# Moving the input layer norm's last step and the query and key evictions from ScalarE to VectorE in an eight-core transformer layer

## The reference, cut to what matters

```
x = x + layernorm(attn(layernorm(x)))          # x: 8 x 2048 x 1024
x = x + layernorm(ffn(layernorm(x)))

attn(x): q, k, v = x @ Wq, x @ Wk, x @ Wv      # 16 heads of 64, causal, ALiBi bias
         softmax(q k^T / 8 + bias) v @ Wo
ffn(x):  z = layernorm(x) * g + b
         top 2 of 8 experts by softmax(z @ rW), weights w
         x + sum_e w_e * (gelu(z @ W1_e + b1_e) @ W2_e + b2_e)
layernorm(x) = (x - mean) / sqrt(var + 1e-5)
```

## Time and profile before

| what | us |
|---|---|
| median of 3 runs | 3216.63 |
| lowest and highest of them | 3211.04, 3339.13 |
| profiled execution, its own time | 3214.51 |
| span of the profiled execution, slowest core (core 6) | 3213.0 |
| spans of the 8 cores | 3193.7 to 3213.0 |
| TensorE busy in the span | 2759.6 (86%) |
| VectorE busy | 907.9 (28%) |
| ScalarE busy | 1045.9 (33%) |

### The profile page before, as it was taken

The page is one execution under the profiler, slowest core; times in us unless marked ns, Lnnn a source line. Parts: engine busy times, 40 slices in busy tenths (PEclk is TensorE's granted clock), DMA queues, the critical chain, the costliest instruction groups (busy, mean ns, idle before and its releaser), DMA issues.

```text
span 3213.0 us, 40015 instructions; the slowest of 8 cores (3193.7 to 3213.0 us)
## 1 busy us (share of the span) xinstructions
PE 2759.6 (86%) x11328; PEld 1411.6 (44%) x18304; DVE 907.9 (28%) x1765; ACT 1045.9 (33%) x2101; POOL 64.7 (2%) x78
## 2 busy tenths in 40 slices
PE   1988888888988643699999999998599999999996
PEld 1555543222222222345555555554255555555553
DVE  4325244545556456310110011004120011011004
ACT  3313656656655466412112211221202211211221
POOL 0000000000000000000000000000000000000000
PEclk9996555555555676799999999999799999999998
DMA  5111000000000532436335543644726534634542
GB/s 145 27 27 27 1 1 1 1 1 1 1 1 1 111 132 105 107 58 105 66 58 88 85 73 53 105 79 108 148 34 105 79 58 75 105 62 62 87 79 92
DMA packets 92893, 205.06 MB, mean 64 GB/s; under 512 B 4248, under 2 KB 12568, under 8 KB 92704
## 3 DMA queue, kind: packets, MB, share of 16 engines
q0 software_dynamic: 75952, 142.64, 27.8%
q1 hardware_dynamic: 16752, 59.85, 5.7%
HBM read 319.96 MB, written 25.17 MB: 107 GB/s over the span
## 4 chain that ended last, share of the span: by engine, by line
PE 77%; DVE 7%; DMA 7%; ACT 4%; issue 4%; DVEq 1%; ACTq 1%; SPq 0%
PE pb L949 27%; PE pb L983 25%; PE pb L475 10%; PE pb L441 9%; PE pb L330 3%; DVE recf_s L503 2%; PE pb L378 2%; DMA x1r<-xuscr 1%; ACT slabs L449 1%; DMA y<-outb 1%; DMA x0t<-x 1%; DMA xpp<-x 1%; PE pb L525 1%; DVE outb L911 1%; DVE st L602 1%
## 5 line engine op out<-in xcount | busy, mean ns | idle before, releaser
L949 PE MATMUL pb<-Trz,fsl 128*128 128x512 bf16 x4013 | 899.6, 383 | 7.5 <-DVE accB L997 2.6
L983 PE MATMUL pb<-fsl,hidT 128*128 128x512 bf16 x4014 | 887.6, 380 | 16.5 <-DVE accB L997 8.6
L957 ACT ACTIVATE hidT<-pb,b_s 128x512 bf16<-128x512 f32 x512 | 323.6, 683 | 1388.2 <-PE pb L949 1388.1
L449 ACT ACTIVATE slabs<-pb,alibi_s 128x512 bf16<-128x512 f32 (+2 forms) x896 | 449.0, 552 | 376.8 <-PE pb L441 376.8
L949 PEld LDWEIGHTS pb<-Trz,fsl 128*128 128x128 bf16 x4096 | 396.8, 97 | 165.2 <-issue 8.1
L983 PEld LDWEIGHTS pb<-fsl,hidT 128*128 128x128 bf16 x4096 | 396.1, 97 | 162.2 <-issue 2.3
L475 PE MATMUL pb<-slabs,vgD 128*65 128x512 bf16 (+5 forms) x818 | 341.0, 510 | 57.0 <-DVE slabs L457 56.9
L441 PE MATMUL pb<-qT,kT 64*128 64x512 bf16 (+2 forms) x896 | 319.6, 472 | 59.9 <-ACT slabs L449 47.2
L994 DVE SCALAR_TENSOR_TENSOR accA<-pb,wS,accA 128x512 f32<-128x512 f32 x64 | 48.1, 751 | 1095.3 <-PE pb L983 1095.0
L942 PEld LDWEIGHTS <-fsl 128*128 128x128 bf16 x2048 | 202.4, 99 | 255.9 <-issue 20.8
L976 PEld LDWEIGHTS <-hidT 128*128 128x128 bf16 x2048 | 201.0, 98 | 257.6 <-issue 18.1
(11 more groups left out here) (110 smaller groups left out, 1189.3 us busy)
## 6 DMA issues: line engine op xcount, KB each, us to landing
fsl<-W POOLq DMA_DIRECT2D x64, 2048.0 KB, 16.0
xpp<-x SPq DMA_DIRECT2D x8, 1024.0 KB, 5.0
x0t<-x SPq DMA_DIRECT2D x16, 512.0 KB, 3.6
xuscr<-x1t SPq DMA_DIRECT2D x16, 512.0 KB, 2.6
xuscr<-ut SPq DMA_DIRECT2D x16, 512.0 KB, 2.6
x1r<-xuscr SPq DMA_DIRECT2D x8, 1024.0 KB, 7.4
y<-outb SPq DMA_DIRECT2D x8, 1024.0 KB, 4.3
accA<-xuscr SPq DMA_DIRECT2D x8, 512.0 KB, 5.3
```

The source lines that it names most:

```text
L449: e.activation(slab, sb[:, 0:qw], AF.Exp, bias=bias, scale=0.125),
L949: tw=tw: e.matmul(b[:, 0:tw], lw, rhs, start=(cc == 0), stop=(cc == CCH - 1)),
L957: e.activation(dst, b[:, 0:tw], AF.Gelu, bias=b1_s[:, e_ * FCH + fc: e_ * FCH + fc + 1], scale=1.0),
L983: e.matmul(b[:, 0:512], lw, rhs, start=(fc == 0), stop=(fc == FCH - 1)),
```

## The change

Three edits. In the input stage the normalise becomes one VectorE operation, (x - mean) * rstd with two per-row scalars, added right behind ScalarE's Ln and Exp of the same block; ScalarE's other three activations go. The load of x, the transposes and the projections wait for VectorE's count where they waited for ScalarE's; the statistics' own wait for ScalarE goes. In `qk_proj` each eviction is a VectorE copy with a drain ahead of it.

```
                     in_=x_in[tc * 128:(tc + 2) * 128, :].rearrange("(two p) c -> p two c", p=128)),
-                    waits=[(sACT, p0_norm_act.get(tc - 3, 0))], inc=sSD, amt=16)
+                    waits=[(sDVE, p0_norm_act.get(tc - 3, 0))], inc=sSD, amt=16)
...
             dve_st = S.add("vector", stats0,
-                           waits=[(sSD, sd_x), (sACT, p0_norm_act.get(tc - 2, 0))], inc=sDVE)
-
-            def rsq0(e, sp=sp, z1=z1, xb=xb):
+                           waits=[(sSD, sd_x)], inc=sDVE)
+
+            def rsq0(e, sp=sp):
                 e.activation(sp[:, 14:15], sp[:, 13:14], AF.Ln, bias=epsv[:, 0:1], scale=1.0)
                 e.drain()
-                e.activation(sp[:, 15:16], sp[:, 14:15], AF.Exp, bias=0.0, scale=-0.5)
-                e.drain()
-                e.activation(sp[:, 16:17], sp[:, 12:13], AF.Copy, bias=0.0, scale=-1.0)
-                e.drain()
-                e.activation(sp[:, 17:18], sp[:, 16:17], AF.Copy, bias=0.0,
-                             scale=sp[:, 15:16])
-                e.drain()
-                return e.activation(z1, xb, AF.Identity, bias=sp[:, 17:18],
-                                    scale=sp[:, 15:16])
-            act_nm = S.add("scalar", rsq0,
-                           waits=[(sDVE, dve_st), (sTE, p0_tr_te.get(tc - 3, 0))], inc=sACT)
+                return e.activation(sp[:, 15:16], sp[:, 14:15], AF.Exp, bias=0.0, scale=-0.5)
+            act_rq = S.add("scalar", rsq0, waits=[(sDVE, dve_st)], inc=sACT)
+
+            def nrm0(e, sp=sp, z1=z1, xb=xb):
+                e.drain()
+                return e.tensor_scalar(z1, xb, sp[:, 12:13], sp[:, 15:16],
+                                       ALU.subtract, ALU.mult)
+            act_nm = S.add("vector", nrm0,
+                           waits=[(sACT, act_rq), (sTE, p0_tr_te.get(tc - 3, 0))], inc=sDVE)
             p0_norm_act[tc] = act_nm
...
-                        waits=[(sACT, p0_norm_act[tc]), (sSD, SD_CONST)] +
+                        waits=[(sDVE, p0_norm_act[tc]), (sSD, SD_CONST)] +
...
-                            a_ev = S.add("scalar", lambda e, b=PB[2 * (tp % 2) + half], d=d:
-                                         e.copy(d, b[:, 0:512]),
-                                         waits=[wr[bids[half]]], inc=sACT)
-                            rd[bids[half]] = (sACT, a_ev)
+                            d_ev = S.add("vector", lambda e, b=PB[2 * (tp % 2) + half], d=d: (
+                                e.drain(), e.tensor_copy(d, b[:, 0:512]))[-1],
+                                waits=[wr[bids[half]]], inc=sDVE)
+                            rd[bids[half]] = (sDVE, d_ev)
```

## The result

| what | before | after |
|---|---|---|
| median of 8 runs each, us | 3216.77 | 3251.37 |
| ratio, 95% interval | | 1.0105 [1.0091, 1.0119] |
| profiled execution, us | 3214.51 | 3250.06 |
| its span, slowest core | 3213.0 | 3248.5 |

The changed kernel is about 1% slower: 34 us by the ratio, 34.6 by the medians. The ratios leave out executions in which a part of the chip ran at a lower clock; the medians don't. The difference is under the 2% that bounds the prediction's three chances, but the whole interval lies above 1. The prediction was 3248.5 us.

The account below looks back on a forecast made before the run. The prediction took TensorE to hold most of the kernel, with the input stage waiting for loads held up by ScalarE's normalise. 15.5+18.5=34.0 us on the profiled 3214.5 gave 3248.5, range 3232 to 3266.

Parts of the forecast that it names:

- three chances: Whole kernel: faster by over 2% 0.01, within 2% 0.93, slower by over 2% 0.06.
- The normalise: Input stage: one VectorE normalise takes 0.812 us, bounds 0.69 and 1.285.
- The trip to ScalarE: Input stage, each block: VectorE waits for ScalarE's Ln and Exp, 0.92 us from the aggregate's start plus 0.15 back.
- Loads out of the way: Input stage: a pair of blocks takes 8.2 us against a load of 5, so the wait for loads goes.
- rival of a stage still paced by loads: Input stage: loads still pace it, its added cost is hidden, only 18.5 us is paid, 3233; chance 0.07.
- First projection matmul: End of the input stage: first projection matmul at 104.2 us instead of 88.66, +15.5 us.
- thirteen steps: Input stage: 13 steps of 4.12 us from the start of block 2 to that of block 15.
- Evictions: Query and key projections: 64 VectorE copies of 0.687 us, 1.5 us per pair due every 3.5, costing 0 us.
- The memsets in their new place: Between keys and values: 25.64 us of VectorE memsets now stand behind all 64 evictions and delay the values, +18.5 us.
- The Wv load: Ahead of the values: rival that VectorE's memsets hold back this GpSimd-issued load, 2 us lost, 3250.5; chance 0.05.
- The clock: Value stage: rival that TensorE's clock stays at 0.50 through 248 matmuls after idling, +47 us, 3295.5; chance 0.05.
- The sum: Whole kernel: 15.5 us in the input stage plus 18.5 us ahead of the values, 34.0 us; chance 0.80.

Follow-up runs that it names:

- e11_norm_twice: The changed kernel with the normalise done twice per block; first query matmul 13.5 us later, total 3260.9 us (one run).
- e5_norm_pipe: The changed kernel with each normalise added behind the next block's statistics; first query matmul at 99.2 us against 103.9, its one total, 3271.4 us, not used.
- e7_evict_twice: The changed kernel with each query and key eviction copy done twice; lower of two totals 3247.1 us.
- e12_fill_f32: The changed kernel with the two big memsets written as float32 over the same bytes; stop ahead of the values 16.6 us, single total 3231.4 us.
- e3_fill_first: The changed kernel with the value tiles' memsets moved ahead of the query projection; 3248.2 us, ratio 1.0092.
- e4_fill_spread: The changed kernel with the memsets cut into 32 pieces, one behind each pair of evictions; 3229.8 us, ratio 1.0027.

## Why the prediction was right, point by point

- **The normalise.** Taken at 0.812 us from line 688; measured 0.812 (16 of them, 13.0 us). A bf16 destination changes nothing.
- **The trip to ScalarE.** Taken at 0.92+0.15 from the aggregate's start; VectorE's timeline has 50.60-49.58=1.02, for the sum of 1.07. The block came to 4.08 us for 4.12.
- **Loads out of the way.** Right: one wait of VectorE for a load, the first. `e11_norm_twice` shows the slack from the other side. The rival of a stage still paced by loads is out for the changed kernel, but it came true in `e5_norm_pipe`, where the normalise is a block later.
- **First projection matmul.** Predicted 104.2; the median core has 103.9, the core of the profile 103.9. Two small misses cancel here: the thirteen steps take 97.38-44.14=53.2 us for 53.6, and from the end of the last normalise to the matmul it is 103.90-100.58=3.3 us for 2.94. The difference itself was taken from 88.66 on core 6; from median to median the input stage costs 103.9-87.2=16.7 us for 15.5, within the bounds given.
- **Evictions.** Taken at 0.687 us from an add; measured 0.692. That they cost nothing, and would cost nothing at twice the number, is shown by the projections' 112.7 us and by `e7_evict_twice`.
- **The memsets in their new place.** Predicted 25.64 us from the last eviction, and a stop of some 27; measured 27.3. That the recorded idle time belongs to the memset was argued, and `e12_fill_f32` shows it; without the 3.52 us the big memset would have been taken a fifth too short.
- **The Wv load** (the rival that VectorE holds it back): it was asked for at 217.1 and took 10.7 us, all of it under the memsets of 218 to 244. Over the eight cores it took 8.1 to 11.0 us there, and 8.3 to 10.3 in the kernel before, with no memsets beside it. Not held back. That took part of the second cost off, as the sum had it.
- **The clock.** The rival said that TensorE might stay at half clock after a stop of 27 us. Two stretches behind the stop, to be compared with the earlier trace rows:

```profile
243.80:247.80 4.00, 3.98 (x10) 1.91 (x21) 0.25 (x2) 0.00 (x0) 0.00 (x0) 0.50 0.00 0
247.80:252.00 4.20, 4.20 (x21) 2.64 (x39) 2.76 (x21) 0.00 (x0) 0.00 (x0) 1.00 0.00 0
```

  Four us at 0.50, the 1.2 GHz level, and then 2.4 GHz: a stop of 27 us costs the same slow start as one of 8.6. The threshold that the prediction gave for this rival, a clock that isn't back within some 35 us of restarting, is too low: at 0.42 us a matmul for 0.22, 30 us are lost over 150 matmuls, which take 63 us. With 4 us measured it changes nothing.
- **The sum.** 15.5+18.5=34.0. Measured on the medians 34.6, on the two profiled executions 35.6. At the start of attention, median to median, it is 16.7+18.4=35.1.
- **A slip.** The prediction counts four ScalarE operations fewer per block; it names three, and three go. Nothing was worked out from the number.

No step failed. The one that could have been sharper is the spread: the input stage's cost was given 10 us of doubt upwards (7.6+2.4), and the durations used were within 5%, but for the 0.4 us of the tail.

## What to carry to other kernels

On an engine that works strictly in order, an instruction moved to it brings along its place in the queue: look at what now stands behind it and who waits for that, not only at whether the engine has time to spare. A step that hands a value to another engine and takes the result back in the same block turns a throughput into a latency; add the next block's work between the two, and then check that the buffers let the loads keep up. Where an engine has only short gaps, a long fill hides in them only if it is cut to their size, as `e3_fill_first` and `e4_fill_spread` show; before, it hid in one piece, because nothing was due on VectorE behind it.

## What the runs showed that was not expected

- Moving the memsets ahead of the projections saves nothing (3248.2 against 3251.4): the stop only changes its place, from 27.3 us at one end to 18.1 us at the bank wait and 9.7 at the load. The expectation of that run had it so, but the idea that any earlier place is better would have been natural.
- In `e5_norm_pipe` the pairs of blocks are hardly shorter than in the changed kernel (7.8 to 8.1 us for 8.2), and some two of the 4.7 us that the start gained come from the first two blocks. A single pair can mislead: on core 6 they range from 7.6 to 8.7 us.
